# A graph attention layer on one core: the first adjacency load is released by another semaphore

## The reference, cut to what matters

```python
e = layernorm(x) @ a1 + (in2 @ a2).T            # 4096 x 4096
e = where(e > 0, e, 0.2 * e)
att = softmax(where(adj > 0, e, NEG), axis=1) * sum(adj, axis=1)
x = x + (0.1 * att + 0.9 * adj) @ in2           # adj is 4096 x 4096, zeros and ones
x = x + layernorm(x) @ weight.T + bias
```

## Time and profile before

| | us |
|---|---|
| median of 3 runs | 386.07 |
| lowest and highest of these | 382.92, 387.5 |
| the profiled execution | 384.71 |
| span of the profiled execution, first to last instruction | 382.9 |

### The profile page before, as it was taken

How to read it: one execution, slowest core, us unless ns; L and a number is a source line. 1 busy time by engine, 2 the same in 40 slices (tenths; PEclk the granted TensorE clock), 3 DMA queues, 4 the chain that set the end, 5 groups by cost and what they waited for, 6 DMA issues and landing times.

```text
span 382.9 us, 8936 instructions
## 1 busy us (share of the span) xinstructions
PE 361.9 (95%) x3231; PEld 317.2 (83%) x3231; DVE 312.1 (81%) x791; ACT 248.3 (65%) x630; POOL 129.0 (34%) x257
## 2 busy tenths in 40 slices
PE   6668999999999999999999999999999999999991
PEld 5557888888888888888888888888888888888880
DVE  5989979959999678976978778897969789899843
ACT  4999966586947293846749193956749198678310
POOL 4485212703443250606144160705325040401021
PEclk9999999999999999999999999999999999999997
DMA  7999959590837999989789998989496830000000
GB/s 242 212 219 218 214 135 185 101 197 30 167 96 19 210 67 189 82 95 178 77 193 19 189 86 160 111 83 189 46 224 19 172 78 14 16 16 15 2 29 18
DMA packets 21771, 44.16 MB, mean 115 GB/s; under 512 B 5078, under 2 KB 13020, under 8 KB 21724
## 3 DMA queue, kind: packets, MB, share of 16 engines
q0 software_dynamic: 9216, 33.56, 61.5%
q1 hardware_dynamic: 12508, 9.98, 9.2%
HBM read 74.97 MB, written 2.11 MB: 201 GB/s over the span
## 4 chain that ended last, share of the span: by engine, by line
PE 89%; DMA 5%; POOL 2%; issue 1%; DVE 1%; ACT 0%; POOLq 0%; DVEq 0%
PE acc_y L671 27%; PE acc_u L688 25%; PE acc_v L691 25%; DMA adj_all<-adj 5%; PE acc_v L671 4%; PE acc_u L671 3%; PE small L656 2%; PE acc_u L662 1%; PE acc_v L662 1%; POOL adj_all L364 1%; PE turned L631 1%; PE small L642 0%; POOL pre_s L383 0%; POOL pre_rstd L374 0%; ACT late L529 0%
## 5 line engine op out<-in xcount | busy, mean ns | idle before, releaser
L500 ACT ACTIVATE steep<-s_bc,steep_s 128x256 bf16<-128x256 f32 x512 | 208.0, 495 | 81.2 <-DMA s_bc<-s_rows 71.1
L691 PE MATMUL acc_v<-weights_v,minus 128*128 128x258 f16 x864 | 191.0, 272 | 0.0
L688 PE MATMUL acc_u<-weights_u,plus 128*128 128x258 f16 x864 | 191.0, 273 | 0.0
L671 PE MATMUL acc_y<-weights_y,adj_all 128*128 128x257 f16 x1024 | 117.0, 273 | 7.5 <-DMA adj_all<-adj 6.2
L671 PEld LDWEIGHTS acc_y<-weights_y,adj_all 128*128 128x128 bf16 x1024 | 99.0, 97 | 22.4 <-issue 4.6
L688 PEld LDWEIGHTS acc_u<-weights_u,plus 128*128 128x128 bf16 x864 | 83.5, 97 | 11.6
L691 PEld LDWEIGHTS acc_v<-weights_v,minus 128*128 128x128 bf16 x864 | 84.0, 97 | 11.0
L884 DVE TENSOR_TENSOR plus<-adj_all,steep 128x2048 bf16<-128x2048 bf16 x64 | 78.4, 1225 | 13.6 <-ACT steep L500 13.0
L887 DVE TENSOR_TENSOR minus<-adj_all,plus 128x2048 bf16<-128x2048 bf16 x64 | 78.4, 1226 | 2.2
L406 POOL TENSOR_SCALAR post_var<-post_mv 128x2 f32<-128x2 f32 x15 | 3.2, 213 | 164.3 <-DVE post_mv L948 164.3
L364 POOL DMA_DIRECT2D adj_all<-adj x64 | 36.2, 583 | 6.8 <-DMA plus<-in 4.7
(11 more groups left out here) (106 smaller groups left out, 308.1 us busy)
## 6 DMA issues: line engine op xcount, KB each, us to landing
adj_all<-adj POOLq DMA_DIRECT2D x64, 512.0 KB, 14.5
x_pre<-x SPq DMA_DIRECT2D x16, 128.0 KB, 10.8
plus<-in SPq DMA_DIRECT2D x4, 512.0 KB, 5.8
x_res<-x SPq DMA_DIRECT2D x16, 128.0 KB, 4.3
out<-late SPq DMA_DIRECT2D x15, 128.0 KB, 3.5
s_bc<-s_rows SPq DMA_DIRECT2D x11, 128.0 KB, 8.3
s_rows<-pre_s SPq DMA_DIRECT2D x11, 1.0 KB
out<-late SPq DMA_DIRECT2D x2, 64.0 KB, 2.3
```

Source lines behind the costliest of these rows:

```text
L500: ins = nc.scalar.activation(steep[:, h, k, :], s1_bc[b][:, :], ACT.Relu, bias=steep_s2[:, jt:jt + 1], scale=STEEP)
L671: ends[t] = nc.tensor.matmul(acc[t][:, 0:width], left[:, jt, cols(t)], right[:, jt, :, :].rearrange("p a b -> p (a b)")[:, 0:width], start ...
L688: last_u = nc.tensor.matmul(acc_u[t][:, 0:2 * WC], plus[b][:, jt, cols(t)], w_u[:, jt, :, :].rearrange("p a b -> p (a b)"), start=(jt == 0 ...
L691: last_v = nc.tensor.matmul(acc_v[t][:, 0:2 * WC], minus[b][:, jt, cols(t)], w_v[:, jt, :, :].rearrange("p a b -> p (a b)"), start=(jt == ...
```

## The change

One wait of GpSimd names another semaphore. The first quarter of the adjacency matrix is requested when the 1 KB row of attention vectors has landed, and not when the first quarter of in2 has.

```diff
-            pool.wait_ge(in2_landed[0], 16)
+            pool.wait_ge(a_landed, 16)
             load_adj(0, (0,))
             row_sums(0, 0)
             load_adj(0, (1, 2, 3))
```

## The result

In 20 runs of each, the changed kernel took 388.24 us in the median (386.0 to 392.57) and the kernel before 385.08 (382.92 to 387.59). The ratio is 1.0074, with a 95% interval of 1.0048 to 1.010: 2.85 us slower on 385.08. The profiled execution after took 388.19 with a span of 386.4, where before it was 384.71 and 382.9 (+3.5).

What follows compares the result with a forecast made beforehand. TensorE's gapless start, held by adjacency quarters and in2's chain, was taken as the bound. In2 landing 6.0 us later, less 1.80 of cover (4.14), less 1.14, gave +3.0: 389.1 on 386.07, range 385.0 to 391.8.

Steps and rivals of the forecast that it cites:

- The 389.1: Whole kernel: the forecast median in us, +3.0 on 386.07; chance 0.42 for +1.9 to +3.8.
- The bound and the two covers: Opening: TensorE's gapless start decides; VectorE's idle 1.80 and TensorE's 1.14 wait absorb part of in2's 6.0 us lateness.
- The request: GpSimd's start: the first adjacency request moves from 6.14 to 2.3 to 2.4 us.
- the seven others: GpSimd behind row_sums: the seven further adjacency requests start near 6.3, not at 9.11 us.
- The first packet: GpSimd's DMA queue: first packet 2.45 us after its request, so at 4.8 instead of 8.6.
- The price of an in2 packet: Shared DMA engines: 0.38 us per in2 packet during the first adjacency quarter, 0.45 behind it, against 0.175 alone.
- shares by bytes: Rival, shared DMA queues: in2 lands near 13.7, +0.5 us, 386.6; chance 0.14 with its neighbours.
- The landing: End of in2's DMA: last quarter lands at 16.2 instead of 10.15 us, 6.0 later.
- the 1.0 for the slowest engine and the receipt: End of in2's DMA: 1.0 us from the mean engine's last packets, near 15.2, to the landing.
- What is hidden behind: Behind the opening: masks keep 1.4 us of room, chunk 2's request moves to about 32, covered by 6.
- The clock, rival 4: TensorE's wait for the maximum of s2 grows to 6 us, the clock halves: +1.9 more, 391.0; chance 0.08.

Runs made afterwards that it cites:

- e1: Changed kernel, but GpSimd waits for in2's second quarter before requesting the seven further adjacency quarters; ratio 1.0057 to the kernel before.
- e4: Kernel before, but SyncE requests in2's last quarter only when the third has landed, adjacency requests as they were; ratio 1.0133.
- e10: The changed kernel itself, timed and profiled once more; ratio 1.013 to the kernel before, median 389.34 us.
- e5: Changed kernel without any wait ahead of GpSimd's first adjacency request; ratio 1.0106 to the kernel before.
- e8: The kernel of e1, unaltered, in a second profiled execution; 387.38 us.
- e3: Changed kernel with 18 filling matmuls behind y of chunk 0 quarter 0, in TensorE's wait for the maximum of s2; ratio 1.0144 to the kernel before.
- e9: Changed kernel with 18 filling matmuls behind y of chunk 0 quarter 0 and 18 behind quarter 3; ratio 1.0054 to the kernel before, median 386.53 us.
- e6: Kernel before with GpSimd's row_sums ahead of its wait for in2's first quarter, so all eight adjacency requests stand together; ratio 0.9984.
- e7: Kernel before with the first adjacency request waiting for in2's second quarter, not its first; ratio 1.0008.
- e12: The kernel of e1 with 18 and 14 filling matmuls behind quarters 0 and 3 of chunk 0's y; ratio 1.0012 to the kernel before.

## Why the prediction was right, and where it was not

The time was right (+3.0 forecast, +2.85 in the 20 runs, +3.5 in the profiled execution), and so was the way to it from in2's landing on; how in2 came to be that late was right in kind and not in its terms. The 389.1 stood on 386.07, the median of 3 runs; on the 385.08 of 20 it would have been 388.1, and 388.24 was measured. Point by point:

- *The bound and the two covers.* Right. The chain from L537 to Y was put at 14.15 and is 14.0 in eight profiles. The covers, 1.80 and 1.14 in the forecast and 2.9 together, came to 3.4: with L 3.45 late (e1) the gapless stretch is 0.07 late, with L 6.67 late it is 3.31. e4 shows that in2's lateness does it without any early request.
- *The request.* 2.3 to 2.4 was forecast, 2.30 measured; the seven others 6.3 against 5.64, as row_sums took 1.3, not 2.15, with VectorE mostly idle beside it.
- *The first packet.* Wrong. I carried the lag of 2.45 over and put it at 4.8; it came at 6.4, 4.1 after the request.
- *The price of an in2 packet.* Too low, 0.38 and then 0.45. From 6.5 to 14.5 in2 sent 1.03 MB, some 250 packets of 4 KB or 15.6 for each engine in 8 us: 0.51. That the queues take turns was right (282 and 312 packets, and 108 and 110 from 9 to 12, behind the slow start of GpSimd's queue), against shares by bytes. The Trainium skill ("DMA: Bandwidth & Descriptors", Queues, rings and completion order) has each DMA engine go round its queues by packets, and the trace agrees in the counts. What the page calls a packet typically holds 9 to 17 descriptors; how long one turn is no view here shows.
- *The landing.* These errors work against each other: fewer in2 packets were left when sharing began (16, not 24.7), each dearer. With 0.51 they end near 14.6 on the mean engine, and with the 1.0 for the slowest engine and the receipt that would be 15.6. The third term was off as well, and not by a fixed amount: the last 8 of in2's 512 packets start from 14.5 to 16.0 in the profile after and from 13.4 to 14.2 in e10's, so most of what parts their landings (16.83 and 15.00; 16.2 was forecast) lies in the few packets that are sent last. A right sum from three wrong terms is luck. In e5 the first packet did come at 4.6, and L was still 16.31.
- *What is hidden behind.* Right. Masks weren't late (39.04 + 1.21 against 41.47, 1.2 of room, 1.4 forecast), chunk 2's request stood at 32.04 (about 32), and nothing waited for it.
- *The clock, rival 4.* The mechanism was there and its place was not. It fell in the wait for the maximum of s2, as said, and y(0,1) to y(0,3) ended near 29.0, in time for linear_part, at no cost; I had priced 1.9 for the case that they ended at 31.6, though 31.6 against VectorE's 29 is 2.6, and no run had that case. The price is paid one wait later, and only in some executions: in e8, e4 and e3, where TensorE had been idle for 2.77, 3.11 and 4.62 ahead of y of chunk 1, the clock was at 1.2 GHz during the first half of that product, which took 1.6 more; in e9, e1, the profile after, e10 and e5, with 0.60 to 2.32, it wasn't. The length of the wait alone doesn't decide it: ahead of y of chunk 0 in e8 TensorE idled 2.86 and the clock stayed up (1.93 for the quarter). Nor is a fall in the opening peculiar to a late in2: it fell from 13.9 to 17.3 in e6 and from 12.7 to 16.1 in e7, where it cost nothing. Filling both waits took 2.5 off the changed kernel (e9 against e10), and 0.45% off e1's (e12, in another set). I had this rival at 0.08 and as an alternative; it comes on top, in some executions.

What stays open: 1.6 is the most that a profile shows for the clock, and e9 is 2.5 to 2.9 under e10. The changed kernel was 1.0074 in one set of runs and 1.013 in another, and one timed run reached 395.76. No profile here caught such an execution. The wait near 320 (0.47 to 2.16 over the profiles, for a copy of ScalarE) is a part of the scatter, in kernels on both sides. Why a few in2 packets come so late, and why the first packet's lag varies, no run shows.

## What to carry to other kernels

A transfer that is requested earlier isn't moved into free time when the DMA engines are full, as they were here: it takes turns with what is under way, and the small load with a long chain behind it (in2) pays for the big one with none. Before moving a request, ask which transfer it will alternate with, and how much later than now that one may land; here it was 3.4 us, and the change took 4.8 to 6.7. TensorE's clock can also be down one wait further on than where one looked for it, so look at it in every wait that grows, and if you fill one, look at the next.

## What the runs showed of the hardware

- The lag from GpSimd's request to the first packet of its queue wasn't constant: 2.5 in the kernel before, 4.1 in the changed one, 4.2 and 4.7 with the same request in e1 and e8, 2.8 in e5, and 1.5 in e7, with in2 all but sent. In e4 the request stands where it does in the kernel before (6.12 and 6.14) and only in2's last quarter isn't queued yet; the lag is 1.5 there, too. But e5, with all of in2 to come, has less than e1, so how the lag goes with what is queued stays open. The Trainium skill ("DMA: Bandwidth & Descriptors", Specifications) gives about 1 us to the first byte on this path; every lag here, counted from the start of a request that itself takes 0.80, is longer. Once on the way the queue needed 2 to 3 us to reach its rate (66 packets in the first 3 us of e5, 159 in 3.2 us later on).
- In both queues' turns each engine sent an in2 packet of 4 KB every 0.51 us, more than the sum of 0.175 (in2 alone) and 0.29 (an adjacency packet).
- A clock held through one wait needn't hold in the next: with a filler in the first wait alone the 48 matmuls of y of chunk 1 took 7.14 us (e3), with fillers in both 5.49 (e9). One program can have either without any filler (5.49 in e1, 7.14 in e8).
